# A token mixer and a mixture of experts on one core: the mixer cut into rounds of four tiles, with the first part of the shared expert inside it

## The chip, the cores and the metric

The kernel runs on one core of a Trainium2 chip. The metric is the device time of one launch in microseconds (us). Inputs and the output lie in DRAM, and all numbers are 32-bit floats. The engines are TensorE (PE, matmuls and transposes into the eight PSUM banks), VectorE (DVE), ScalarE (ACT), GpSimd (POOL) and SyncE (SP), which here only issues transfers. Each engine runs its own list of instructions in the order in which the program wrote them, and waits on semaphores.

## The reference, cut to what matters

Two sequences of 1024 tokens (16 tiles of 128 tokens) with 512 features pass through two layers.

```python
h = layernorm(x) * (1 + ca) + sa
x_shift = (roll(h, -T//2) @ Wts.T) * g + h * (1 - g)
xn = layernorm(x_shift) * ln_w + ln_b
k, v = xn @ Wk.T, xn @ Wv.T
wkv = exp(-exp(time_first) * sigmoid(k)) * v
states: s = s * exp(time_decay) + wkv          # a scan over the tokens
x = x + ga * (states @ Wo.T)
h = layernorm(x) * (1 + cb) + sb
shared = (silu(h @ Wsg) * (h @ Wsu)) @ Wsd * sigmoid(h @ Wse)
# router: softmax(h @ Wr), best 4 of 32 experts per token, at most 64 tokens
# per expert; each expert is silu(xe @ Wg) * (xe @ Wu) @ Wd
x = x + gb * (shared + weighted sum of the token's expert rows)
```

The hidden width of the shared expert is 1408, that of one routed expert 352.

## The kernel before, in words

The program has two blocks, and no engine begins the second before the first has ended on all.

**The mixer block** takes one sequence (8 tiles) at a time. First come eight `mixer` products (L884: 12 matmuls each, since a 32-bit product is made of three products of high and low parts in the fp32r type), and behind each `mix_front` on DVE (L723, then statistics L690 to L696), a power on POOL (L378), the normalization L713, a transpose on PE (L837), its copy on ACT (L467) and the low part on DVE (L594). Two `keys_values` products of 12 matmuls each (L899) and two scans (`kv_scan`, L732 and L734) follow. Then come eight `project` products (L923) with `residual` on DVE (L740, L690 to L696, L749), a scaling on ACT (L502), an addition on POOL (L404) and a transpose. `router` (L915) makes the logits of four tiles at a time. The second sequence repeats this.

**The expert block** runs 16 `UNITS` (p, g) in order: part p of the shared expert's width (2, 3, 3 and 3 chunks of 128) for group g of four tiles. A unit is, for each chunk, `gate_up` (24 matmuls, L1557) with silu on ACT (L1241) and a product on DVE (L1432), then four `down` products (L1570: 9 matmuls for three chunks, 6 for two) with two DVE instructions each (L1453, L1456). In unit 0 DVE also picks the experts; PE then counts the places (`positions`, L1640 and L1641) and DVE makes the indices (`slots`, L1384 to L1409) and signals `route_ok`. POOL writes 64 columns of token numbers by indirect transfers (L1181), SP reads the table back (L1123), and POOL gathers the rows of the first pair of experts (L1188). The 16 pairs have three stages each on PE: `pair_rows` and `pair_gate_up` (L1589, L1601: 32 matmuls), `pair_turned` (L1607), `pair_down` (L1618: 12 matmuls). One stage stands behind each chunk and each down of units 5 to 11 (`stage_after`), 49 places for 49 stages. A pair's weights lie in one buffer each: SP loads `egu` (four transfers of 704 KB, L1108) when the pair before has done `pair_gate_up`, then `ed` (two of 512 and two of 192 KB, L1112 and L1113) when it has done `pair_down`, then stores the pair's output `ye` (256 KB, L1136) and waits for that store (L1138) before it looks at the next pair. The last four units run beside the gather and sum of the experts' rows, which POOL issues (L1206).

## Time and profile before

| | us |
|---|---|
| median of 3 runs (lowest, highest) | 864.04 (861.78, 864.19) |
| span of the profiled execution | 815.9 |
| PE busy in it | 705.4 |
| DVE busy in it | 433.8 |
| POOL busy in it | 287.8 |
| ACT busy in it | 219.7 |

No time of its own is recorded for the profiled execution beside its span; the median run is 48.1 us longer than the span, which is what lies ahead of the first instruction and behind the last. A busy PE is not PE at its peak: the records of matmuls overlap, and they are longer where the granted clock is lower.

### The profile page before, as it was taken

What the parts mean: (1) busy time and instruction counts of PE and PEld (TensorE: products, weight loads), DVE (VectorE), ACT (ScalarE), POOL (GpSimd) and SP (SyncE); (2) the same over time, 40 slices, a digit from 0 to 9 for tenths busy, and PEclk for the clock granted to TensorE, in tenths of its full rate; (3) what the DMA queues carried; (4) which work ended last, traced back from release to release, by engine and by line L of the source; (5) the groups of instructions that cost most, each with busy time, mean ns of one, the idle gap of its engine ahead of it and who ended that gap; (6) DMA issues with size and microseconds to landing.
All of it is one profiled execution on the core that took longest, in us unless ns stands there. A gap on an engine that the chain in (4) does not pass through costs nothing.

```text
span 815.9 us, 8820 instructions
## 1 busy us (share of the span) xinstructions
PE 705.4 (86%) x3153; PEld 478.0 (59%) x3153; DVE 433.8 (53%) x749; ACT 219.7 (27%) x402; POOL 287.8 (35%) x272
## 2 busy tenths in 40 slices
PE   5798687978874899937999999999999999896995
PEld 3666534852252676825666566657566666674773
DVE  2888587647378766620323234241413234677777
ACT  2423423123241223301213132222223241322420
POOL 0184636813322377760000000000000002888881
PEclk9799756978697999977999999999999999998998
DMA  8610011021130430003685858668876763521111
GB/s 283 252 56 1 0 40 64 1 77 39 64 117 0 140 75 1 0 14 135 233 319 181 308 163 297 252 225 312 314 271 224 268 224 108 151 70 40 39 41 64
DMA packets 50487, 111.49 MB, mean 137 GB/s; under 512 B 11392, under 2 KB 15508, under 8 KB 50444
## 3 DMA queue, kind: packets, MB, share of 16 engines
q1 hardware_dynamic: 41996, 102.48, 35.6%
q0 software_dynamic: 8448, 8.46, 3.9%
q8 instruction: 25, 0.41, 0.2%
q14 instruction: 18, 0.15, 0.1%
HBM read 110.84 MB, written 12.62 MB: 151 GB/s over the span
## 4 chain that ended last, share of the span: by engine, by line
PE 38%; POOL 11%; DVE 9%; issue 8%; DMA 4%; ACT 1%; SPq 1%; POOLq 0%; DVEq 0%; ACTq 0%
PE bank L1557 16%; PE bank L1601 9%; POOL slot_tokens L1181 7%; PE bank L1570 6%; PE bank L1618 5%; POOL egu L1206 2%; DMA egu<-in_L_ffn_Wu_dram 2%; DVE ytmp L1470 1%; PE bank L1589 1%; DMA expert_rows<-ye 1%; DMA xg<-h_rows,slot_tok 1%; DVE xsL L1425 1%; DVE egu L1366 1%; DVE prod L1432 1%; PE bank L1607 1%
## 5 line engine op out<-in xcount | busy, mean ns | idle before, releaser
L1557 PE MATMUL bank<-xsH,wguH 128*128 128x512 f32 x352 | 142.3, 404 | 9.1 <-DVE xsL L1425 6.7
L1557 PE MATMUL bank<-xsH,wguL 128*128 128x512 f32 x352 | 138.5, 393 | 0.0
L1557 PE MATMUL bank<-xsL,wguH 128*128 128x512 f32 x352 | 138.4, 393 | 0.0
L1188 POOL DMA_INDIRECT xg<-h_rows,slot_tok x16 | 16.0, 999 | 273.5 <-PE bank L1589 270.5
L1432 DVE TENSOR_TENSOR prod<-bank,silu 128x512 f32<-128x512 f32 x44 | 30.4, 690 | 154.0 <-PE bank L1557 142.0
L1570 PE MATMUL bank<-wdH,prodH 128*128 128x512 f32 x176 | 75.1, 427 | 28.7 <-DVE prodL L1434 14.5
L1557 PEld LDWEIGHTS bank<-xsH,wguH 128*128 128x128 f32 x352 | 67.1, 191 | 30.8 <-issue 7.8
L1181 POOL DMA_INDIRECT slot_tokens<-tok_id,t_idx x64 | 67.8, 1060 | 43.1 <-DVE slotw L1409 23.9
L1601 PE MATMUL bank<-egu,xeT 128*64 128x352 f32 x512 | 79.3, 462 | 1.8 <-DMA egu<-in_L_ffn_Wu_dram 1.7
L1557 PEld LDWEIGHTS bank<-xsL,wguH 128*128 128x128 f32 x352 | 66.8, 190 | 14.5
L1557 PEld LDWEIGHTS bank<-xsH,wguL 128*128 128x128 f32 x352 | 67.0, 190 | 13.7 <-issue 0.7
L1570 PE MATMUL bank<-wdL,prodH 128*128 128x512 f32 x176 | 70.7, 402 | 0.0
L1570 PE MATMUL bank<-wdH,prodL 128*128 128x512 f32 x176 | 70.7, 402 | 0.0
L1243 ACT ACTIVATE prodH<-prod 128x512 fp32r<-128x512 f32 x44 | 27.8, 631 | 134.0 <-DVE prod L1432 134.0
L1570 PEld LDWEIGHTS bank<-wdH,prodH 128*128 128x128 f32 x176 | 34.3, 195 | 47.1 <-DVE prodL L1434 17.4
L1601 PEld LDWEIGHTS bank<-egu,xeT 128*64 128x64 f32 x512 | 36.6, 137 | 40.7 <-issue 32.9
L1241 ACT ACTIVATE silu<-bank 128x512 f32<-128x512 f32 x44 | 26.3, 597 | 120.4 <-PE bank L1557 120.2
L1206 POOL DMA_INDIRECT egu<-expert_rows,y_idx x44 | 50.0, 1136 | 19.5 <-issue 12.1
L1453 DVE SCALAR_TENSOR_TENSOR ytmp<-bank,sigma,gate_b 128x512 f32<-128x512 f32 x48 | 35.9, 747 | 31.0 <-PE bank L1570 30.7
L884 PE MATMUL bank<-wtsH,hT 128*128 128x512 f32 x128 | 47.1, 430 | 0.0
L1434 DVE TENSOR_TENSOR prodL<-prod,prodH 128x512 fp32r<-128x512 f32 x44 | 30.5, 692 | 30.7 <-ACT prodH L1243 30.7
L378 POOL TENSOR_TENSOR rs<-ve,neg_half 128x1 f32<-128x1 f32 x32 | 20.8, 651 | 69.7 <-DVE ve L696 69.7
(217 smaller groups left out, 1121.2 us busy)
## 6 DMA issues: line engine op xcount, KB each, us to landing
egu<-in_L_ffn_Wg_dram SPq DMA_DIRECT2D x32, 704.0 KB, 6.6
egu<-in_L_ffn_Wu_dram SPq DMA_DIRECT2D x32, 704.0 KB, 7.9
ed<-in_L_ffn_Wd_dram SPq DMA_DIRECT2D x32, 512.0 KB, 5.4
h2T<-in_L_wmod_dram SPq DMA_DIRECT2D x6, 1024.0 KB, 8.5
ed<-in_L_ffn_Wd_dram SPq DMA_DIRECT2D x32, 192.0 KB, 6.3
xres<-in_L_attn_x_dram SPq DMA_DIRECT2D x4, 1024.0 KB, 13.4
h_rows<-h2r SPq DMA_DIRECT2D x16, 256.0 KB, 2.0
expert_rows<-ye SPq DMA_DIRECT2D x16, 256.0 KB, 7.0
```

What stands on the lines that cost most here:

```text
L884: ins = m.matmul(sbk[i % 2][:, :], l[:, c, s * P:(s + 1) * P], r[:, c, :], start=(k == 0), stop=(k == 3 * C - 1))
L1181: gp.indirect_dma_start(tok_dram[:, :], bass.IndirectOffsetOnAxis(t_idx[:, i, k:k + 1], axis=0), tok_id[:, i:i + 1], None, bounds_check=E ...
L1206: gp.indirect_dma_start(yg[i % NY][:, k, :], None, ye_dram[:, :], bass.IndirectOffsetOnAxis(y_idx[:, i, k:k + 1], axis=0), bounds_check=E ...
L1241: a.activation(silu[:, :], gB[:, :], ACT.Silu).then_inc(silu_ok, 1)
L1243: a.activation(prodH[:, f, :], prod[:, :], ACT.Copy).then_inc(phi_ok, 1)
L1432: v.tensor_tensor(prod[:, :], uB[:, :], silu[:, :], ALU.mult).then_inc(prod_ok, 1)
L1434: v.tensor_tensor(prodL[:, f, :], prod[:, :], prodH[:, f, :].bitcast(F32), ALU.subtract).then_inc(plo_ok, 1)
L1453: v.scalar_tensor_tensor(ytmp[:, m % 2, :], dB[m % 2][:, :], sigma[:, i:i + 1], gate_b[:, i // BT, :], ALU.mult, ALU.mult).then_inc(d_used ...
L1557: ins = mm.matmul(bk[:, :], l[:, w, c, at], r[:, c, :], start=(k == 0), stop=(k == 3 * C - 1))
L1570: ins = mm.matmul(dB[m % 2][:, :], l[:, f, m * P:(m + 1) * P], r[:, f, :], start=(f == 0 and k == 0), stop=(f == nf - 1 and k == 2))
L1601: ins = mm.matmul(bk[half, 0:F], xeT[:, c, half], egu[:, e, w, c, :], start=(c == 0), stop=(c == C - 1))
L1618: ins = mm.matmul(eyB[half, :], epT[0:n, c, half], ed[0:n, e, c, :], start=(c == 0), stop=(c == len(FC) - 1))
```

## The change

The two blocks become one. The mixer runs in five rounds g of four tiles: round g has the `mixer` products of group g (rounds 0 to 3) and, step by step between them, the `project` products of group g - 1 (rounds 1 to 4); a round ends with `keys_values(g)` and `router(g - 1)`. Units (0, 0) to (0, 2) of the shared expert stand in rounds 2, 3 and 4 (`early_piece`). All products of the mixer share two PSUM banks in turn, so a `mixer` product of rounds 1 to 3 waits until DVE has taken the one before it. `keys_values` is 4 plain fp32 matmuls on undivided operands, which drops the 16 low parts of `xnT` on DVE. The router's operands change sides (16 matmuls of 34 columns), so that the logits come with tokens on partitions. A chunk of a unit is cut into halves of 12 matmuls. The pairs' 49 stages are spread over 44 places from unit 7, place 6, to the end of unit 11. SP asks for the third part's weights ahead of the scatter and not behind it. Buffers of the mixer and of the experts lie over each other, with waits that keep them apart.

```text
unit:    0-2          3          4 5 6    7 ... 11            12-15
before:  after mixer  --------   5 to 11: 49 stages           sum of rows
after:   in rounds    routing    scatter  7 (place 6) to 11   sum of rows
```

```diff
-    PAIR_UNIT = NG + 1
+    EARLY = NG - 1
...
-                    def keys_values(b, n):
...
-                        for c in range(C):
-                            for l, r in ((kvH, xnTH), (kvH, xnTL), (kvL, xnTH)):
-                                ins = m.matmul(kvb[:, :], l[:, c, :], r[:, c, :], start=(k == 0), stop=(k == 3 * C - 1))
-                                k += 1
-                        ins.then_inc(kv_full, 1)
...
-                if u < PAIR_UNIT:
-                    return None
-                n = sum(steps(UNITS[w][0]) for w in range(PAIR_UNIT, u)) + k - 1
-                j, stage = n // 3, n % 3
...
-                    load_part(1)
-                    sp.wait_ge(route_ok, 1)
-                    load_gate_up(0)
-                    load_down(0)
-                    sp.wait_ge(scat, 16 * NT * TOP_K)
...
-                        if j == 0:
-                            load_part(2)
-                        if j == NP // 2 + 1:
-                            load_part(3)
...
+        PAIRS_FROM = (7, 6)
+        PLACES = [(u, k) for u in range(PAIRS_FROM[0], MERGE) for k in range(2 * PARTS[UNITS[u][0]] + GT)
+                  if (u, k) >= PAIRS_FROM]
+        STAGES = 3 * NP + 1
+        stages_at = {}
+        for s in range(STAGES):
+            stages_at.setdefault(PLACES[s * len(PLACES) // STAGES], []).append(divmod(s - 1, 3))
...
+                sp.wait_ge(route_ok, 2)
+                load_gate_up(0)
+                load_down(0)
+                load_part(2)
+                sp.wait_ge(scat, 16 * NT * TOP_K)
+                sp.dma_start(slot_tok[:, :], tok_dram.rearrange("(p j) a -> p (j a)", p=P)).then_inc(tab_in, 16)
...
+                for g in range(NG + 1):
+                    for i in range(GT):
+                        t = g * GT + i
+                        if g < NG and 1 < t + 1 < NT:
+                            h_lo(t + 1)
+                        if g > 2 and i == 0:
+                            down(0, g - 3, 2)
+                            down(0, g - 3, 3)
+                        if g > 1 and i == 0:
+                            lo_group(0, g - 2)
+                            sigma_of(g - 2)
+                        if 2 <= g < NG and i in (1, 2):
+                            gate_up(0, g - 2, i - 1)
+                        if 2 <= g < NG and i == 3:
+                            down(0, g - 2, 0)
+                            down(0, g - 2, 1)
+                        if g == NG and i == 2:
+                            gate_up(0, g - 2, 0)
+                        if g < NG:
+                            mix_front(t)
+                        if g:
+                            residual(t - GT)
+                        if g < NG:
+                            mix_norm(t)
...
+                    for f in range(n):
+                        pair_stages(u, 2 * f)
+                        gate_up(p, g, f)
+                        if u == EARLY and f == 0:
+                            top_experts()
+                        if u == EARLY and f == 1:
+                            experts_mask()
+                        if f == 0 and g == 0 and p:
+                            for k in weights_ahead(u - 1)[2:]:
+                                lo_weights(p, k)
+                            lo_weights(p, n)
+                        if u == POOL_UNIT and f == 0:
+                            positions()
+                            slots()
+                        if u == POOL_UNIT and f == 1:
+                            slot_weights()
+                        pair_stages(u, 2 * f + 1)
...
+                def keys_values(g):
+                    k = product_bank(("kv", g))
+                    for i in range(GT):
+                        turn_taken(pe, ("xn", g * GT + i))
+                    if g == 0:
+                        pe.wait_ge(kvW_ok, C)
+                    for c in range(C):
+                        ins = mm.matmul(s_bank[k][:, :], kvW[:, c, :], xnT[:, c, :], start=(c == 0), stop=(c == C - 1))
+                    ins.then_inc(s_full[k], 1)
...
+                    for i in range(GT):
+                        turn_taken(pe, ("h2", g * GT + i))
+                        for c in range(C):
+                            ins = mm.matmul(s_bank[k][:, i * R:(i + 1) * R], h2T[:, g, c, i * P:(i + 1) * P], wrN[:, c, :],
+                                            start=(c == 0), stop=(c == C - 1))
...
+                    if k < 2 * NC0:
+                        half(0, g, k // 2, k % 2)
+                    else:
+                        down(0, g, k - 2 * NC0)
...
+                for g in range(NG + 1):
+                    for i in range(GT):
+                        t = g * GT + i
+                        for q in before_mixer(g, i):
+                            turn(q)
+                        if g < NG:
+                            mixer(t)
+                        if g:
+                            project(t - GT)
+                        if 2 <= g < NG:
+                            early_piece(g - 2, 2 * i)
...
+                            vector_product(i + 3)
+                        for q in amid(g, i):
+                            turn(q)
+                        if 2 <= g < NG:
+                            early_piece(g - 2, 2 * i + 1)
+                        for q in after_step(g, i):
+                            turn(q)
+                        if g == 0:
+                            vector_columns(i + 3)
+                    if g == NG:
+                        for k in range(GT, 2 * GT):
+                            early_piece(g - 2, k)
+                    for q in before_end(g):
+                        turn(q)
+                    if g < NG:
+                        keys_values(g)
+                    for q in at_end(g):
+                        turn(q)
+                    if g:
+                        router(g - 1)
...
+                    for f in range(n):
+                        half(p, g, f, 0)
+                        pair_stages(u, 2 * f)
+                        half(p, g, f, 1)
+                        pair_stages(u, 2 * f + 1)
+                    for m in range(GT):
+                        down(p, g, m)
+                        pair_stages(u, 2 * n + m)
```

Three places of the order in which the engines' instructions now stand. First DVE, one step of a mixer stage; before, a step of the second sequence (`mix_front`, the normalization of the tile before, a low part):

```order
L723 TENSOR_TENSOR xs<-bank,mix 128x512
L690 BN_STATS st<-xs 128x6
L695 BN_AGGR mv<-st 128x2
L696 TENSOR_SCALAR ve<-mv 128x1
L713 TENSOR_SCALAR xn<-xs,mv,rs 128x512
L594 TENSOR_TENSOR xnTL<-bank,xnTH 128x4x128
```

After, the second step of round 2 (`gate_up` of the shared expert, `mix_front`, `residual`, the normalization `mx`):

```order
L1100 TENSOR_TENSOR silu<-bank,silu 128x512
L1102 TENSOR_TENSOR prodL<-silu,prodH 128x512
L1022 TENSOR_TENSOR mx<-bank,mx 128x512
L1024 BN_STATS st<-mx 128x6
L1027 BN_AGGR mvx<-st 128x2
L1028 TENSOR_SCALAR vex<-mvx 128x1
L1039 TENSOR_TENSOR xres<-bank,xres 128x512
L1041 BN_STATS st<-xres 128x6
L1045 BN_AGGR mvh<-st 128x2
L1046 TENSOR_SCALAR veh<-mvh 128x1
L1056 SCALAR_TENSOR_TENSOR ho<-xres,mvh,bc 128x512
L1033 TENSOR_SCALAR mx<-mx,mvx,rsx 128x512
```

Each step now holds a tile of both stages and a piece of the shared expert, and the low part of `xnT` (L594 on `xnTL`) is gone.

Second DVE, where it makes the experts' places; before, behind the last downs of unit 0:

```order
L1453 SCALAR_TENSOR_TENSOR ytmp<-bank,sigma,gate_b 128x512
L1456 TENSOR_TENSOR xres<-xres,ytmp 128x512
L1384 TENSOR_TENSOR ed<-bank,egu 128x16x32 x4
L1387 TENSOR_REDUCE pos<-ed 128x64
L1389 TENSOR_SCALAR over<-pos 128x64
```

After, at the start of unit 4 (L1100 and L1102 are `gate_up` of its first chunk, L1082 and L1086 low parts of weights, L1173 the first of `positions`):

```order
L1121 SCALAR_TENSOR_TENSOR ytmp<-bank,sigma,gate_b 128x512
L1124 TENSOR_TENSOR xres<-xres,ytmp 128x512
L1082 TENSOR_TENSOR wguL<-wguN,wguH 128x1024
L1100 TENSOR_TENSOR prod<-bank,silu 128x512
L1102 TENSOR_TENSOR prodL<-prod,prodH 128x512
L1082 TENSOR_TENSOR wguL<-wguN,wguH 128x1024
L1086 TENSOR_TENSOR wdL<-wdN,wdH 128x512 x3
L1173 TENSOR_TENSOR ed<-bank,egu 128x16x32 x4
L1176 TENSOR_REDUCE egu<-ed 128x64
```

Compared with before, the places are now made behind the first chunk of the next unit and further low parts of weights.

Third ACT, around the decay factors of a group (L492 to L495 before); before:

```order
L467 ACTIVATE xnTH<-bank 128x4x128 x5
L492 ACTIVATE kE<-bank,kvbias 64x512
L493 ACTIVATE vV<-bank 64x512
L495 ACTIVATE kE<-kE,wcol 64x512
L467 ACTIVATE xnTH<-bank 128x4x128 x3
```

After, from the end of round 2 into round 3:

```order
L704 ACTIVATE kE<-bank,kvbias 64x512
L705 ACTIVATE vV<-bank 64x512
L707 ACT_TABLE_LOAD
L707 ACTIVATE kE<-kE,wcol 64x512
L684 ACTIVATE h2T<-bank 128x4x128
L667 ACTIVATE bc<-bank 128x512 x2
L717 ACTIVATE logits<-bank 128x136
L723 ACTIVATE sigma<-logits 128x4
L672 ACTIVATE hT<-bank 128x512
L754 ACTIVATE xsH<-h2T 128x512 x4
L762 ACT_TABLE_LOAD
L762 ACTIVATE silu<-bank 128x512
```

A table load now stands between `vV` and the exponential, and another ahead of each round's first silu.

## Rows read from the trace of the kernel before

**Rows 1.** Stretches: length, busy PE, PEld, DVE, ACT, POOL, clock, DMA share, GB/s.

```profile
0.00:31.00 31.00, 19.92 (x102) 14.47 (x102) 13.95 (x39) 10.39 (x19) 1.92 (x9) 0.86 0.91 317
31.00:85.00 54.00, 48.76 (x278) 36.88 (x276) 44.82 (x103) 17.22 (x33) 27.78 (x25) 0.95 0.13 41
85.00:133.00 48.00, 36.64 (x97) 20.74 (x98) 34.60 (x62) 17.43 (x30) 26.22 (x23) 0.56 0.08 28
133.00:177.00 44.00, 35.49 (x168) 28.58 (x169) 32.58 (x61) 10.25 (x17) 29.07 (x27) 0.89 0.16 54
177.00:224.30 47.30, 41.37 (x92) 15.57 (x92) 21.71 (x42) 13.99 (x23) 15.12 (x16) 0.72 0.12 45
224.30:275.60 51.30, 33.63 (x129) 24.44 (x130) 43.20 (x105) 12.51 (x20) 10.35 (x15) 0.87 0.14 47
275.60:372.60 97.00, 73.64 (x312) 57.23 (x311) 49.84 (x71) 23.76 (x39) 68.79 (x65) 0.92 0.25 70
372.60:687.20 314.60, 311.81 (x1549) 198.12 (x1550) 101.98 (x147) 80.85 (x171) 18.52 (x16) 0.99 0.68 240
687.20:815.90 128.70, 104.14 (x432) 81.95 (x432) 91.10 (x122) 33.30 (x54) 90.00 (x77) 0.94 0.23 68
```

**Rows 2.** POOL in time: first scatter, first gather.

```profile
275.57 1.25 POOL L1181 DMA_INDIRECT slot_tokens<-tok_id,t_idx  x1 [23.88 <-DVE slotw L1409]
...
365.54 1.00 POOL L1188 DMA_INDIRECT xg<-h_rows,slot_tok  x1 [2.96 <-DMA slot_tok<-slot_tokens]
```

**Rows 3.** PE in time: start us, length us, what; in brackets idle before.

```profile
372.66 1.13 PE L1589 MATMUL bank<-ident,xg 128*128 128x128 f32 x4 [19.47 <-DMA xg<-h_rows,slot_tok]
```

**Rows 4.** The chain that ended last: start us, length us, what.

```profile
262.19 1.71 PE bank L1640 x2
...
265.65 2.49 DVE ed L1384 x4
...
365.54 7.07 DMA xg<-h_rows,slot_tok
...
380.97 4.88 PE bank L1601 x32
...
406.98 2.07 PE bank L1570 x9
409.05 2.73 PE bank L1618 x12
412.46 5.49 PE bank L1557 x24
```

**Rows 5.** DVE groups by form: busy us, mean ns, then idle before.

```profile
L1453 DVE SCALAR_TENSOR_TENSOR ytmp<-bank,sigma,gate_b 128x512 f32<-128x512 f32 x48 | 35.9, 747 | 31.0 <-PE bank L1570 30.7
...
L723 DVE TENSOR_TENSOR xs<-bank,mix 128x512 f32<-128x512 f32 x16 | 11.0, 689 | 13.0 <-PE bank L884 12.6 <-POOL mix L391 0.3
...
L740 DVE TENSOR_TENSOR xres<-bank,xres 128x512 f32<-128x512 f32 x16 | 11.0, 686 | 10.0 <-PE bank L923 9.9
```

**Rows 6.** PE in time, a router product of four fp32 matmuls.

```profile
188.01 3.62 PE L915 MATMUL bank<-h2T,wrN 128*34 128x512 f32 x8
```

**Rows 7.** ACT groups: the table load ahead of the silu.

```profile
L1241 ACT ACT_TABLE_LOAD x1 | 1.3, 1283 | 0.0
```

**Rows 8.** SP's issues in time, one cycle of pair weights.

```profile
446.08 0.34 SPq L1108 DMA_DIRECT2D egu<-in_L_ffn_Wg_dram  x1
...
454.72 0.65 SPq L1136 DMA_DIRECT2D expert_rows<-ye  x1
462.81 0.34 SPq L1108 DMA_DIRECT2D egu<-in_L_ffn_Wg_dram  x1
```

**Rows 9.** PE in time, the pair that waits for its weights.

```profile
456.80 3.47 PE L1601 MATMUL bank<-egu,xeT 128*64 128x352 f32 x22 [1.51 <-DMA egu<-in_L_ffn_Wu_dram]
```

**Rows 10.** The page's 40 slices (20.4 us each): granted clock, GB/s.

```profile
PEclk9799756978697999977999999999999999998998
...
GB/s 283 252 56 1 0 40 64 1 77 39 64 117 0 140 75 1 0 14 135 233 319 181 308 163 297 252 225 312 314 271 224 268 224 108 151 70 40 39 41 64
```

2457 lines of the change are left out of this document (1205 added, 1252 removed).

## The prediction

> **What bounds the kernel now.** I read the stretches first, since four parts of the program have different limits. The mixer block takes 224.3 us, and no engine is full in it: DVE is busy 44.82 of 54 us while the first sequence is mixed, but only 34.60 of 48 and 21.71 of 47.3 in the two `project` stretches, and the granted clock falls to 0.56 there [rows 1]. PE and DVE wait for each other along one chain. Next comes routing, 51.3 us, which is DVE's. Then POOL scatters: from 275.57, when it has waited for DVE's last index, to the first gather at 365.54 [rows 2]. PE has finished units 1 to 4 by then and sits idle 19.47 us until the gathered rows land at 372.66 [rows 3]. The pairs take 314.6 us, 311.81 of them with PE busy and a full clock [rows 1]. The last 128.7 us are POOL's gathers (90.00 us busy) with PE at 104.14.
>
> Check of the PE-bound part by counting: 24 matmuls of a chunk take 5.49, nine of a down 2.07, 32 of `pair_gate_up` 4.88, 12 of `pair_down` 2.73 [rows 4]. A three-chunk unit is 3 x 5.49 + 4 x 2.07 = 24.8; a pair with its transposes (about 1.2) is 8.8. From 372.66 before had two chunks, four downs, six units and 16 pairs: 19.3 + 148.8 + 141 = 309, against 314.6 measured. So the counting holds to 2%.
>
> **The change, part by part.** I follow four points of time: M, the end of the last router product (224.3 before, taken as the end of the mixer stretch [rows 1]); the first gathered rows on PE; the last `pair_down`; the end.
>
> *M.* Work that moves in: three units of part 0 (72 matmuls, 16.4 us of PE each, 49 in all), and on DVE 12 low parts at about 0.7, 12 products and low parts of `gate_up`, 12 downs of two instructions and the weights' low parts, 38 us at about 0.7 each [rows 5]; 16 low parts of `xnT` at about 0.7 go, so +27. DVE was busy 147.7 us up to 224.3 (sum of the first five lines of [rows 1]); it would be 175. At the old density (0.66) M would be 265, at the 0.83 of the best stretch 211. By steps: round 0 is half of the old 54 us, from 31 to 58. Its end then lies open: `keys_values` in fp32 (four matmuls as in [rows 6], 3.6 instead of 2.7), the decay factors, the scan, the gate columns: 12, so 70. Round 1: a step has about 17 DVE instructions, at the 0.435 mean and 0.83 density of the 54 us stretch 8.9 each, so 105. Rounds 2 and 3: PE's step is a mixer product (2.74), a projection (0.9, one fp32 matmul as in [rows 6]), two halves (5.5) and transposes (1), 10.2; the two steps with downs are DVE's, 9 each. Between rounds PE goes through `keys_values`, transposes and the router product (3.6 each, [rows 6]) and DVE through scan, downs and low parts before the next `mix_front`; I count 12 to 15 us per round end, so 50 and 53 per round: 155, 208. Round 4 has no mixer, eight pieces of 16.4 us behind four projections, and two products at its ends: 46. M = 254, bounds 240 (PE's work alone at full clock, with no wait at the ends) and 272.
>
> *Table loads.* The order shows eight instead of two. One takes 1.28 us [rows 7]. Those ahead of the silu fall into ACT's wait for a gate product; two stand between `vV` and the exponential, on the chain of the scan: 2.6, inside the 53s. The Trainium skill (ScalarE: Activation LUTs, "What ACT_TABLE_LOAD costs") gives about 2.66 us per switch, drain included. The trace shows only the 1.28; by the page six further switches, all exposed, would cost 16.
>
> *M to the first gathered rows.* Before, 372.66 - 224.3 = 148.4. Up to `positions` the chain keeps its length (the block's start and the logits' copies go, a low part comes). Before, DVE began the places at 265.65 [rows 4] and POOL scattered at 275.57 [rows 2]. After, DVE first needs both halves of unit 4's first chunk (5.5), their product, high and low part (2.2), and four low parts (3.4): about 11, less 1.2 for `slotw`, which now comes later. So +10. Against it, part 2's weights no longer stand in front of the first gather, whose landing took 7.07 [rows 4]; I take 2.5 for it, -4.6. So +5.6, bounds 0 and +10. PE has units 4 to 6 and most of 7 to do meanwhile, 74 + 18.5 from M + 41, and the rows come at M + 154: it idles about 17, much as before. Moving the pairs to unit 7 therefore costs nothing here.
>
> *The pairs.* What is left for PE from there: three downs of unit 7 (6.2), units 8 to 11 (99), 16 pairs (141): 246. But `pair_gate_up` must start every 15.6 us on average (14.2 to 16.9 by the places), where before it was 19.7. SP's cycle of one pair, where it was packed, ran from 446.08 to 462.81 [rows 8]: the load of `egu`, 10.7 us until PE could start at 456.80 after a wait of 1.51 [rows 9], 4.95 of matmuls, and the wait for the store of `ye`, issued at 454.72 behind `ed`. So 16.7 is the period that the single buffers and SP's order allow. A pair moves 4736 KB (4.85 MB); at the best slice, 319 GB/s [rows 10], that is 15.2. I take 16.3 where PE would be faster: +13 over 15 periods, and +2 for part 3's weights. Pairs 261, bounds 246 (PE) and 272 (16.7 throughout, and 7 for part 3). Gain 314.6 - 261 = 53.6.
>
> The Trainium skill (DMA: Bandwidth & Descriptors, "Bandwidth") puts the ceiling of the SBUF side at 435 GB/s, by which the bytes of a pair need 11.1 us and PE stays the bound, 246 and not 261. No slice here shows more than 319, over 20 us; whether the ceiling is reached inside one is not in these rows.
>
> *The tail.* POOL's gathers follow the last store of `ye` and are not touched: 128.7.
>
> *Sum*, against the span of 815.9: M +29.7, routing +5.6, pairs -53.6, tail 0: -18.3. The span becomes 797.6. The median of the runs is 48.1 above the span, which nothing here changes: 864.0 - 18.3 = 846.
>
> **The rivals.**
>
> *A, faster still.* Pairs at PE's pace (-15) or M at its lower bound of 240 (-14), each alone 831, both 817. For it: DMA share is only 0.68 in the pairs [rows 1], and PE's pieces fill the mixer's waits, so the clock may stay high. Against it: a wait of PE for `egu` is already there at a period of 15.7 [rows 9]. The ceiling rule above would give 831. Chance 0.20.
>
> *B, slower.* The mixer's rounds lock step: each `mixer` product waits for DVE to empty its bank, DVE waits for a projection behind it, and PE's in-order pieces stand in front of the transposes that POOL and DVE wait for. If each of the 12 steps and four round ends of rounds 1 to 4 takes 2.2 us more than I count, M is 289 and the time 881; slower begins at M = 275, 1.3 us each. For it: DVE's density of 0.66 in the old mixer gives 265 with a simpler order. Against it: in the 54 us stretch DVE and PE ran at 0.83 and 0.90 together with such a chain. Chance 0.20.
>
> *C, table loads.* If every one of the six lies on a chain, 6 x 1.28 = 7.7, of which 2.6 are counted: 851; by the skill's 2.66 it would be 859. Chance 0.05.
>
> *D, it comes out even.* The pairs' periods reach only 17.5 (SP late at each store), +18 over 15 periods, with the rest as forecast: 864. Chance 0.07.
>
> **How the numbers follow.** The forecast has 0.48, with its own range of 836 to 857. The range of 8 in 10 reaches to 826 (half of A lies below 831) and to 870 (about half of B beyond). A measurement tells 0.3%, 2.6 us, from no change: faster takes the forecast, A, C and a third of D, 0.75; same 0.05; slower 0.20.
>
> **What would show it.** Right: the last router product at 240 to 272 in the new profile, with DVE at about 0.7 of that stretch; first scatter 60 us or so behind it; PE's wait for `xg` of 10 to 25; `pair_gate_up` starting every 16 to 17 us, with several waits for `egu`; tail 127 to 131. Wrong: M above 275 (B); no wait for `egu` and pairs of 246 (A); ACT's table loads in the chain more than twice (C); SP's waits for the store longer than 8 (D). A tail of another length would break the sum where I put nothing.

## The result, and the profile after

The changed kernel takes 888.61 us (median of four runs, 886.71 to 901.44), the kernel before 863.33: 1.0291 times as long, 95% interval 1.0272 to 1.0309. The longest of the four, a disturbed run, is left out of the ratio. The change makes the kernel slower by 25 us, where 18 less was forecast.

The stretches of the changed kernel's profiled execution (888.17 us, span 886.3), cut at the last router product (M), the first scatter, the first gather, the first gathered rows on PE and the last `pair_down`. They answer to [rows 1]:

```profile
core 0: us, PE busy (x) PEld busy (x) DVE busy (x) ACT busy (x) POOL busy (x), PEclk, DMA share, GB/s
0.00:279.30 279.30, 223.03 (x1029) 159.70 (x1029) 172.82 (x347) 91.08 (x155) 96.01 (x92) 0.88 0.21 73
279.30:341.10 61.80, 40.25 (x137) 29.80 (x138) 44.59 (x104) 16.66 (x27) 7.79 (x13) 0.79 0.00 1
341.10:427.60 86.50, 35.77 (x138) 27.78 (x138) 16.51 (x28) 9.36 (x17) 64.20 (x64) 0.70 0.34 78
427.60:484.60 57.00, 50.67 (x214) 41.45 (x215) 25.44 (x37) 12.25 (x21) 1.00 (x1) 0.91 0.02 5
484.60:758.90 274.30, 251.99 (x1271) 145.79 (x1269) 72.34 (x107) 63.90 (x144) 17.71 (x16) 0.97 0.77 275
758.90:886.30 127.40, 103.98 (x432) 81.97 (x432) 92.60 (x124) 33.21 (x56) 88.70 (x77) 0.94 0.23 69
```

Two things stand out. M is 279.3, not 254. And in the 86.5 us of the scatter PE gets 138 matmuls done, where in the profile before it got 312 done; then it has 50 us of the shared expert left when the gathered rows are there.

The timeline of the scatter (POOL, ACT and DVE rows in order of time; in brackets the engine's idle time before, and its releaser, "remote" where none in the program is found):

```profile
341.12 1.24 POOL L606 DMA_INDIRECT slot_tokens<-tok_id,t_idx  x1 [34.47 <-DVE t_idx L1191]
...
381.80 0.60 ACT L762 ACTIVATE silu<-bank 128x512 f32<-128x512 f32 x1 [11.92 <-remote]
...
412.66 0.69 DVE L1100 TENSOR_TENSOR prod<-bank,silu 128x512 f32<-128x512 f32 x1 [42.03 <-remote]
...
423.55 0.97 POOL L606 DMA_INDIRECT slot_tokens<-tok_id,t_idx  x1 [0.30 <-issue]
427.61 1.00 POOL L613 DMA_INDIRECT xg<-h_rows,slot_tok  x1 [3.09 <-DMA slot_tok<-slot_tokens]
...
432.96 0.75 DVE L1121 SCALAR_TENSOR_TENSOR ytmp<-bank,sigma,gate_b 128x512 f32<-128x512 f32 x1 [17.02 <-remote]
```

ACT takes the gate product of a chunk at 381.80; DVE can take its `up` product, 12 matmuls later in PE's order, only at 412.66: 30.9 / 12 = 2.6 us per matmul of 512 columns, where [rows 4] have 5.49 / 24 = 0.23. The first down ends 15 matmuls further on, at 432.96, 9 us behind the issue of the last scatter. The granted clock can't be the cause: 2.6 is eleven times 0.23, and at the lower of its two levels (0.50 from 341.5 to 345.3 us) these matmuls follow each other by 0.43. I call this the slow stretch. It is the subject of half the experiments, since it hides what the change does.

### The profile page after: what moved, and what is told of

Read it like the earlier page. It is cut to its first block, busy times and chain, and to the rows that moved or that the text cites. A ratio compares the mean times of both kernels' runs of the same rounds, so it can differ in the third digit from the quotient of the medians.

```text
span 886.3 us, 8906 instructions
## 1 busy us (share of the span) xinstructions
PE 705.7 (80%) x3217; PEld 486.5 (55%) x3217; DVE 424.3 (48%) x745; ACT 226.5 (26%) x418; POOL 275.4 (31%) x263
## 4 chain that ended last, share of the span: by engine, by line
PE 40%; DVE 15%; DMA 14%; issue 10%; another core or an unknown queue 7%; POOL 6%; ACT 4%; SPq 3%; POOLq 0%; DVEq 0%; ACTq 0%
PE bank L1478 16%; DMA egu<-in_L_ffn_Wu_dram 7%; PE bank L1533 6%; DMA expert_rows<-ye 6%; PE bank L1490 6%; PE bank L1428 3%; PE bank L1550 3%; PE bank L1439 2%; POOL egu L631 2%; DMA xres<-in_L_attn_x_dram 1%; DVE ytmp L1212 1%; PE bank L1459 1%; DVE prod L1100 1%; SPq L458 1%
## 5 line engine op out<-in xcount | busy, mean ns | idle before, releaser
L1478 PE MATMUL bank<-xsH,wguH 128*128 128x512 f32 x352 | 144.9, 412 | 16.3 <-DVE xsL L1092 9.4
L1490 PE MATMUL bank<-wdH,prodH 128*128 128x512 f32 x176 | 77.0, 438 | 81.3 <-issue 39.9
L613 POOL DMA_INDIRECT xg<-h_rows,slot_tok x16 | 15.2, 949 | 289.0 <-PE bank L1521 285.9
L1100 DVE TENSOR_TENSOR prod<-bank,silu 128x512 f32<-128x512 f32 x38 | 26.2, 691 | 160.1 <-PE bank L1478 95.7
L1533 PE MATMUL bank<-egu,xeT 128*64 128x352 f32 x512 | 84.6, 486 | 19.8 <-DMA egu<-in_L_ffn_Wu_dram 17.5
L1478 PEld LDWEIGHTS bank<-xsH,wguH 128*128 128x128 f32 x352 | 67.8, 193 | 44.2 <-issue 20.2
L606 POOL DMA_INDIRECT slot_tokens<-tok_id,t_idx x64 | 64.2, 1003 | 53.7 <-DVE t_idx L1191 34.5
L1490 PE MATMUL bank<-wdH,prodL 128*128 128x512 f32 x176 | 72.8, 413 | 0.0
L1533 PEld LDWEIGHTS bank<-egu,xeT 128*64 128x64 f32 x512 | 38.0, 144 | 62.4 <-issue 37.1
L768 ACT ACTIVATE prodH<-prod 128x512 fp32r<-128x512 f32 x38 | 24.0, 631 | 156.7 <-DVE prod L1100 146.5
L1205 DVE TENSOR_TENSOR eprod<-bank,esilu 128x352 f32<-128x352 f32 x16 | 8.4, 525 | 105.1 <-ACT esilu L778 105.1
L1428 PE MATMUL bank<-wtsH,hT 128*128 128x512 f32 x128 | 49.9, 454 | 2.5 <-DVE wtsL L939 1.7
L1550 PE MATMUL bank<-ed,epT 128*64 128x512 f32 (+1 forms) x192 | 44.8, 600 | 0.9 <-issue 0.9
```

Source lines behind the costliest of these rows:

```text
L606: gp.indirect_dma_start(tok_dram[:, :], bass.IndirectOffsetOnAxis(t_idx[:, i, k:k + 1], axis=0), tok_id[:, i:i + 1], None, bounds_check=E ...
L768: a.activation(prodH[f][:, :], src[:, :], ACT.Copy).then_inc(phi_ok, 1)
L1100: v.tensor_tensor(to[:, :], uB[:, :], silu[:, :], ALU.mult).then_inc(prod_ok, 1)
L1428: ins = mm.matmul(s_bank[k][:, :], l[:, c, :], r[:, c, :], start=(n == 0), stop=(n == 3 * C - 1))
L1478: ins = mm.matmul(bk[:, :], l[f][:, w, c, :], r[:, c, :], start=(k == 0), stop=(k == 3 * C - 1))
L1490: ins = mm.matmul(dB[m % 2][:, :], l[f][:, m * P:(m + 1) * P], r[f][:, :], start=(f == 0 and k == 0), stop=(f == nf - 1 and k == 2))
```

## The experiments

Ratios are to the kernel before, run beside it on the same chip, with 95% intervals. The experiments ran on four chips, so two of them from different chips are compared by these ratios and not by their times. Where a stretch is given, it is from the run's own profile, one execution. How far that can be trusted, M shows: in the seven profiles of the changed kernel in which nothing ahead of M is altered it lies between 277.3 and 282.8.

### Where the 48 us outside the span were

**before_again**: the kernel before, unchanged.

> The kernel before, unchanged, to see in one execution both its span and its own time. The changed kernel's execution lay 1.9 us outside its span (888.17 against 886.3), while for the kernel before 48 us were left over between a span of 815.9 and runs of 864. Theory 1 (the profile shown of before was an execution in which TensorE was not held up while the scatter ran, and the timed runs have such a stretch): a span of about 861 us here, 1.9 us below its own time, with a hold-up of TensorE of some 45 us between the first scatter and the first gathered rows. Theory 2 (the 48 us really lie outside the span of this kernel): a span of about 816 us beside a time of about 864.

862.43 us, ratio 0.9986 [0.9957, 1.0014]; its profiled execution took 864.01 with a span of 862.2. Theory 1. Its stretches from M on (columns as above):

```profile
223.10:275.20 52.10, 33.62 (x129) 24.46 (x130) 43.21 (x105) 13.12 (x21) 10.37 (x15) 0.87 0.14 46
275.20:360.20 85.00, 24.02 (x90) 17.81 (x89) 11.28 (x17) 5.36 (x10) 62.86 (x64) 0.68 0.20 52
360.20:421.30 61.10, 54.25 (x222) 42.85 (x223) 37.34 (x52) 17.76 (x28) 1.00 (x1) 0.92 0.13 44
421.30:733.90 312.60, 309.49 (x1550) 196.33 (x1548) 103.31 (x149) 81.41 (x171) 18.53 (x16) 1.00 0.68 241
```

Only 90 matmuls run in the scatter, and the pairs begin at 421.3, where [rows 3] have 372.66. The profile shown of before was of an execution without the slow stretch; the timed runs, by their times, have it. So my 48.1 us "outside the span" were 1.8 us outside it and 46 of slow stretch. Against this execution the change reads: M +56.2, routing to the first scatter +9.7, scatter and the work behind it -2.6, pairs -38.3, tail -0.9: +24.1.

### What the slow stretch is

**part2_late**: the third weight group is loaded behind the slot table's read.

```
-                load_part(2)
                 sp.wait_ge(scat, 16 * NT * TOP_K)
                 sp.dma_start(slot_tok[:, :], ...)
+                load_part(2)
```

> The changed kernel with the load of the shared expert's third group of weight columns moved on SyncE from ahead of the read of the slot table to behind it, so that its 2.3 MB are not under way while the scatter runs. In the changed kernel three products of TensorE in the scatter ended 10, 31 and 15 us late, from the moment that these transfers ended. Theory 1 (the hold-up comes with these transfers): it is gone, first gathered rows are used at about 434 instead of 484, time about 840 us. Theory 2 (it has to do with the scatter itself or with TensorE's own activity): the hold-up of 50 to 60 us stays, time 885 to 892.

889.98, 1.0303 [1.0253, 1.0352]: nothing changes (138 matmuls in the scatter again), theory 2.

**half_scatter**: `for i in range(NT // 2)` around the scatters, so the second sequence's tokens get no slot.

> The changed kernel that leaves out the last 32 of the 64 scatters, so the second sequence's tokens are in no slot (their experts' part is not computed; the gathers read other rows in their place, with the same number of transfers). The scatter ends 41 us earlier. Theory 1 (TensorE is held up until the scatter is over): the slow stretch, which begins 30 us behind the first scatter, lasts to about 392 instead of 433, TensorE reaches the pairs at about 444 instead of 484, and the time is 843 to 850. Theory 2 (the slow stretch has a length of its own and only falls into the scatter): no change of it, time 884 to 890.

847.32, 0.9808 [0.9740, 0.9876]. The last scatter is issued at 381.5 instead of 423.6, and PE is at the pairs at 436.0 instead of 484.6, with the same 138 matmuls done between the first scatter and the first gather. Theory 1: the slow stretch ends with the scatters.

**scatter_paced**: four semaphores in turn, and a wait on the one four places back.

```
+                        q = i * TOP_K + k
+                        if q >= 4:
+                            pool.wait_ge(scats[q % 4], 16 * (q // 4))
                         gp.indirect_dma_start(tok_dram[:, :], ...).then_inc(scats[q % 4], 16)
```

> The changed kernel with the 64 scatters of the slot table paced: each waits on GpSimd until the one four places ahead of it has landed, so at most four are under way. All five executions looked at except the one shown of the kernel before have a stretch behind the first 20 to 30 us of the scatter in which TensorE gets one product of 512 columns done in about 2.5 us, two scatters' time, where it takes 0.23. Theory 1 (what holds TensorE up are scatters that pile up unfinished): the products run at 0.23 throughout, TensorE reaches the pairs when the rows land, at about 435, and the time is 838 to 845. Theory 2 (the issuing of a scatter itself, or something else of that time, holds it up): unchanged, 885 to 892, or a little longer if the scatters take longer.

Three runs at 878 to 881 and one at 863. PE gets 203 matmuls done in the scatter and then has the slow stretch: neither theory as it stood, but the pacing moves it.

**scatter_by_two** and **before_by_two**: the same with two in place of four, on either kernel.

> The changed kernel with at most two of the 64 scatters under way (with four, TensorE's slow stretch began 44 us behind the first scatter instead of 30, and one run of four came out at 863). Theory 1 (unfinished scatters are what holds TensorE up): no slow stretch, some 290 products in the scatter instead of 137, pairs begin when the rows land, and the time is 838 to 850, by how much longer the 64 scatters take. Theory 2 (pacing does not matter, and where the stretch begins is chance): 875 to 895, with the slow stretch.

> The kernel before with the same pacing, at most two scatters under way. Theory 1 (the hold-up is the same thing in both kernels, and the execution shown of before was one without it): 815 to 830, that is 15 to 24 us faster than the changed kernel paced alike, so the change's own effect is there without the hold-up too. Theory 2 (the hold-up stays): 855 to 870.

863.65, 0.9957 [0.9922, 0.9991], and 835.47, 0.9650 [0.9587, 0.9713]. The slow stretch is gone in both. The stretch of the scatter in scatter_by_two, columns as above:

```profile
344.70:458.50 113.80, 82.83 (x351) 66.99 (x351) 43.46 (x67) 23.85 (x40) 64.91 (x64) 0.86 0.21 60
```

PE does 351 matmuls, runs out of work and waits 34 us, as the 64 scatters now take 110 us instead of 82. Both times lie above the ranges I gave (838 to 850 and 815 to 830), and I had expected 15 to 24 us between the two, where there are 28. But theory 1 holds, and without the slow stretch the change costs as much as with it. One thing these runs leave open: with two under way the scatters are also issued more slowly, one per 1.74 us instead of 1.31 in the mean, and no run separates the number under way from the rate.

### The pairs

**pairs_early**: `PAIRS_FROM = (6, 6)` instead of `(7, 6)`.

> The changed kernel with the pairs' first stage 10 places earlier in the list of turns, (6, 6) instead of (7, 6), so 54 places for 49 stages. In the changed kernel TensorE comes to the first pair at 484.6, 57 us after the gather was issued at 427.6, with 50 us of the shared expert still ahead of the pairs. Theory 1 (the order keeps the pairs back after a hold-up): the first rows are used some 20 us earlier, at about 462, and of TensorE's 22 us of idle time in the pairs some 5 to 10 go, time 878 to 884. Theory 2 (pairs are bound by their transfers and the tail takes what is saved): no change, 886 to 890. If the hold-up is absent in this execution TensorE waits for the gather instead, and the time is about 840.

870.05 (ten runs, 863 to 885), 1.0036 [0.9999, 1.0072]. The first rows are used at 463.5 (21 earlier), the pairs take 278.1. Theory 1, and more than the 5 to 11 us that its range allowed: with the slow stretch the late start of the pairs leaves PE idle in the pairs (251.99 busy of 274.30 above), with the earlier one it is 271.12 of 278.10.

**sp_order**: SyncE waits for a pair's store behind the next `load_gate_up`.

```
                         load_gate_up(j + 1)
+                    if j:
+                        sp.wait_ge(ye_sent, 16 * j)
+                        sp.sem_inc(ye_free, 1)
...
-                    sp.wait_ge(ye_sent, 16 * (j + 1))
-                    sp.sem_inc(ye_free, 1)
```

> The changed kernel with SyncE waiting for the store of an expert pair's rows one place later, behind the issue of the next pair's gate and up weights instead of ahead of it. In the changed kernel SyncE waits 116 us in all for these stores and TensorE 17.5 us in all for the weights. Theory 1 (the weights come late since SyncE stands at the store): TensorE's wait for them falls below 6 us, and the pairs take 8 to 12 us less, 876 to 880. Theory 2 (the weights are late because TensorE asks for them in bursts and the transfers are at what the memory gives): no change, 885 to 890.

889.32, 1.0293 [1.0236, 1.0350]. The pairs take 262.1 instead of 274.3, as theory 1 says (PE's wait for `egu` falls to 8.0, not below 6); the total does not move, since PE came to the pairs at 494.8. Nothing ahead of that differs in the order of any engine's work, and yet the slow stretch began earlier: 95 matmuls in the scatter instead of 138.

**combo**: (6, 6), this order of SyncE, and two edits of the mixer told below.

> The changed kernel with four edits together: pairs from (6, 6), SyncE's later wait for the store, the order of round 1, and the rows ahead in round 2. The stretches that these moved when made alone: M -5.8 (round 1's order), 0 to -6 (rows ahead), pairs 274.3 to 262.1 (SyncE's wait), and 17 us by the earlier pairs. Theory 1 (they add up as far as TensorE has idle time left; it has 7 us in the pairs with the earlier start): M at 268 to 273, the pairs 272 to 276, time 855 to 862, even with the kernel before or a little faster. Theory 2 (the slow stretch in the scatter gives it back, as it did in the two runs with one edit): 868 or more.

869.34, 1.0017 [0.9988, 1.0047]; theory 2. 107 matmuls in the scatter. From here on I paced by two.

**combo_by_two**: this order of SyncE and round1_order below, `PAIRS_FROM` unchanged.

> The changed kernel with at most two scatters under way, the order of round 1 and SyncE's later wait for the store. Made alone these took 5.8 us from M and 12.2 from the pairs, and neither run was faster, since the slow stretch in the scatter began 10 us earlier in both. Theory 1 (that was chance): without the slow stretch both come through, 863.65 - 18 = 846, range 843 to 849. Theory 2 (something downstream takes back what they give, such as the last transfers or the tail): 855 or more.

843.25, 0.9757 [0.9712, 0.9802], against 0.9957 for scatter_by_two: theory 1, both gains come through (M 272.9, pairs 260.7). PE's waits in its pairs (total, times, longest):

```profile
PE bank L1531 <- DMA xg<-h_rows,slot_tok: 35.2, 1, 35.2
PE bank L1543 <- DMA egu<-in_L_ffn_Wu_dram: 5.7, 4, 4.2
```

The waits of PE and of SyncE's queue in the changed kernel's pairs, where PE's wait for `egu` was 17.5:

```profile
PE bank L1533 <- DMA egu<-in_L_ffn_Wu_dram: 17.5, 9, 9.2
...
SPq L491 <- DMA expert_rows<-ye: 114.1, 15, 12.6
```

### The mixer

**no_pieces**: none of the shared expert in the rounds, its first three units behind the mixer. One unit's low part is made of another group's rows here, so its part of the output is not the reference's; the operations are the same in kind and number.

> The changed kernel with none of the shared expert's first part inside the mixer's rounds: its first three units are computed behind the mixer, with the fourth, and the routing's vector work stands beside units 0 and 1; the load of the third group of columns stands behind the read of the slot table. The three units take 72 products each, 3 x 72 x 0.227 = 49 us of TensorE. Theory 1 (the rounds are bound by TensorE's order of work, and the pieces cost there what they cost alone): the last router product ends at 279 - 49 = 230. Theory 2 (the rounds are bound by the chain through VectorE, ScalarE and GpSimd from step to step, and the pieces lie in its gaps): it ends at 260 or later. In between, each us of pieces cost (279 - M)/49. As the same work stands behind the mixer, the whole is 886 to 895 with the hold-up of TensorE in the scatter, and about 840 to 850 without it.

932.53, 1.0796 [1.0746, 1.0845]. M is 259.2: taking 49 us of PE's work out gives back 20, so about 30 of the 49 lay in gaps; between the theories. The total is beyond both, as the slow stretch took the time in which PE would have done this work.

**no_pieces_by_two**: the same, with each group's own rows, paced.

> The changed kernel with at most two scatters under way and with the shared expert's first three units behind the mixer instead of in its rounds. Beside scatter_by_two (863.65; M at 282.8, first scatter at 344.7, TensorE idle for 34 us before the gathered rows, pairs at 462). Theory 1 (the pieces cost nearly half their own 49 us in the rounds, and TensorE could do them in its idle time under the scatter): M at 259, first scatter at about 315, rows at about 435, TensorE busy until about 445, pairs from there: 845 to 850, faster than with the pieces. Theory 2 (the pieces in the rounds pay): TensorE comes to the pairs later than 462, and the time is 865 or more.

859.50, 0.9950 [0.9921, 0.9980], beside 0.9957 for scatter_by_two. M 262.2, first scatter 318.2, PE at the pairs at 458.1 against 462.0. Neither theory: the time is the same, since PE had 27 us left behind the gather, where I had reckoned 10. With the scatters paced, running the pieces beside the mixer is worth nothing: what PE saves there it idles away under the scatter. Unpaced it was worth 44 us (932.5 against 888.6).

**round1_order**: on DVE the statistics ahead of the weights' low parts, on POOL `first_rstd` behind `mix_rows`.

```
-                            if i < NC0 + 1:
-                                first_lo(i)
                             for q in FIRST[2 * i:2 * i + 2]:
                                 first_stats(1, q)
...
+                            if i < NC0 + 1:
+                                first_lo(i)
```

> The changed kernel with two places of round 1 in another order: on VectorE a step's statistics of the second sequence come ahead of the low parts of the shared expert's first weights, so that ScalarE's copy of those weights (1.8 to 1.9 us of VectorE's waiting, three times) lies beside them; on GpSimd the power of the second sequence's variances comes behind mix_rows and h2_rows instead of ahead of mix_rows (VectorE waited 3.2 us for mix_rows there). Theory 1 (round 1 is bound by one chain through VectorE and GpSimd, and such waits stand on it): 5 to 8 us shorter up to the last router product, 271 to 274 instead of 279, time 880 to 884. Theory 2 (the chain only waits elsewhere): no change, 886 to 890.

Round 1, from its first sum to its last norm, takes 37.9 us instead of 46.9, and the end of the round behind it is no longer than before. M is 273.5 (5.8 less, and below all seven profiles with the old order), theory 1; the total, 892.84, 1.0273 [1.0202, 1.0345], is lost to a longer slow stretch (83 matmuls in the scatter).

**rows_ahead**: `first_rows` ahead of `mix_front` in round 2.

> The changed kernel with VectorE writing the second sequence's normalised rows ahead of mix_front in the steps of round 2, instead of behind mix_norm. In round 2 TensorE's turn ('h', t + 1) waits for these rows, which wait for mix_norm(t), which waits for TensorE's mixer product of t, so the two engines take turns. Theory 1 (this turn-taking sets the step of round 2): round 2, from the keys and values of group 1 to those of group 2, takes 50 to 54 us instead of 57.4, and the last router product ends at 273 to 276. Theory 2 (TensorE's pieces set it): 57 us and 279. The whole moves by as much, if the slow stretch in the scatter begins where it did.

901.27, 1.0408 [1.0344, 1.0472]; round 2 takes 57.2 us (57.4 without the edit), M is 283.5. Theory 2. So the turn-taking of DVE and PE within a step does not set the pace of round 2.

**router_late**: the router's products of groups 0 and 1 behind the next round's first mixer product (paced).

> The changed kernel with at most two scatters under way and the router's products of groups 0 and 1 one place later in TensorE's order, behind the first mixer product of the next round instead of ahead of it. Theory 1 (VectorE's first sum of rounds 2 and 3 is late since the mixer product stands behind 32 products of the router, 6.7 us, of TensorE): the gaps from the last norm of a round to the first sum of the next shrink from 20.2 and 27.9 by 3 to 6 us each, M by 5 to 10, time 854 to 859 beside 863.65. Theory 2 (TensorE is full there, and what is moved comes back in the step behind): the gaps shrink but M moves by less than 3.

870.01, 1.0076 [1.0046, 1.0106], 1.2% above scatter_by_two's 0.9957. The gap from round 2's norm to round 3's sum falls from 27.9 to 20.5, and the step behind it grows from 9.0 to 17.4; M is 289.0, where 282.8 was without the edit. Theory 2, and worse.

**front_first**: DVE's `mix_front` ahead of the low parts and the downs at the rounds' starts (paced).

> The changed kernel with at most two scatters under way and VectorE's first step of rounds 2 and 3 in another order: mix_front first, then the low parts of the piece's group and sigma, then the two downs that were left, then residual and mix_norm (before: downs, low parts, sigma, mix_front, residual, mix_norm). Theory 1 (the next round's first sum waits for what stands ahead of it on VectorE): the gap from round 2's last norm to round 3's first sum falls from 27.9 to about 24.5, M from 282.8 to 277 to 280, time 858 to 861 beside 863.65. Theory 2 (TensorE's order sets the pace there, and the pieces' first half now starts later): the gap falls, the step behind grows by as much, M and time move by less than 2.

870.05, 1.0051 [1.0014, 1.0088], 0.9% above scatter_by_two. The gap falls to 24.8, the step grows to 14.8; M is 285.1. Theory 2 again, and slower.

### A version that beats both

**before_late_pairs**: before_by_two with the pairs' 49 stages from unit 6 on, and the SyncE order above.

> The kernel before with at most two scatters under way, the pairs' 49 stages spread from the third place of unit 6 (two units and two places of work of TensorE are then ahead of the first pair instead of one unit) as the changed kernel spreads them, and SyncE's later wait for the store. Beside before_by_two (835.5, TensorE idle for 39 us before the gathered rows). Theory 1 (TensorE has the work for its idle time, and the pairs then run at the transfers' pace of 16.4 us each): pairs start at about 390 and take 270 to 280 instead of 314, time 795 to 805. Theory 2 (the denser pairs wait for transfers): pairs take 290 or more, 812 to 825.

829.65, 0.9585 [0.9508, 0.9661]. Theory 2: the pairs take 308.8, and the time lies above even that theory's 812 to 825. PE is idle for 26.5 us of them, 17.8 for `egu` (not the 40 that the next expectation names).

**before_fine_pairs**: with the changed kernel's places, one behind each half of a chunk.

```
+            PLACES = [(u, k) for u in range(6, NG * (len(PARTS) - 1))
+                      for k in range(2 * PARTS[UNITS[u][0]] + GT) if (u, k) >= (6, 4)]
...
-                            pair_stage(u, f)
+                            pair_stage(u, 2 * f + 1)
```

> before_late_pairs (829.65; pairs 308.8 us, of which TensorE waited some 40) with the places of the pairs' stages as the changed kernel has them: one behind each half of a chunk and one behind each down, ten in a unit, from the fifth of unit 6. Theory 1 (with one place behind a whole chunk, 5.5 us of products, several stages of a pair fall together, so that TensorE asks for weights in bursts): the pairs take 262 to 276, time 790 to 800. Theory 2 (the transfers' pace beside the mixer of before is what it is): the pairs stay above 300, time 825 to 832.

804.47, 0.9268 [0.9219, 0.9316]. Its stretches from the first scatter on, cut as before:

```profile
274.60:387.40 112.80, 106.59 (x456) 84.23 (x455) 63.45 (x91) 31.41 (x52) 68.81 (x64) 1.00 0.14 40
387.40:394.50 7.10, 0.00 (x0) 0.00 (x0) 0.00 (x0) 0.00 (x0) 1.00 (x1) 0.55 0.98 338
...
394.50:679.10 284.60, 278.57 (x1396) 168.05 (x1396) 85.67 (x124) 73.05 (x157) 18.52 (x16) 0.99 0.74 265
679.10:808.00 128.90, 108.33 (x442) 85.60 (x441) 93.54 (x124) 33.30 (x54) 89.86 (x77) 0.93 0.22 68
```

PE is busy 106.59 of the 112.80 us of the scatter and 278.57 of the 284.60 of the pairs, so they are PE's again, not the transfers'. Theory 1, somewhat short of it (262 to 276 for the pairs and 790 to 800 in all were expected). The old mixer, paced scatters, SyncE's later wait and the changed kernel's way of spreading the pairs are together 7.3% faster than before.

## Why the prediction was wrong

**The sum.** 846 was forecast, 888.6 measured: 42.6 too low. M +25.3 (279.3 for 254); M to the first gathered rows +51.3 (205.3 for 154); pairs +13.3 (274.3 for 261); tail -1.3 (127.4 for 128.7); outside the span -46.2 (1.9 for 48.1). The second and the last are the same thing, the slow stretch, counted in the profile on one side and outside the span on the other: they nearly cancel, +5.1. That is luck: I took 46 us of slow stretch for a constant, and the changed kernel happens to have one of its own. What turned the sign is M, and the pairs with it.

**M = 254, the step that failed.** The steps can be set beside the profile with DVE's first sum (L1022) of a round and the last norm (L1033):

```profile
56.46 1.48 DVE L1033 TENSOR_SCALAR mx<-mx,mvx,rsx 128x512 f32<-128x512 f32 x1 [0.66 <-POOL rsx L529]
...
71.76 0.69 DVE L1022 TENSOR_TENSOR mx<-bank,mx 128x512 f32<-128x512 f32 x1 [1.36 <-PE bank L1428]
...
118.08 0.54 DVE L1033 TENSOR_SCALAR mx<-mx,mvx,rsx 128x512 f32<-128x512 f32 x1
...
138.84 0.69 DVE L1022 TENSOR_TENSOR mx<-bank,mx 128x512 f32<-128x512 f32 x1 [0.51 <-PE bank L1428]
...
175.42 0.54 DVE L1033 TENSOR_SCALAR mx<-mx,mvx,rsx 128x512 f32<-128x512 f32 x1
...
203.90 0.69 DVE L1022 TENSOR_TENSOR mx<-bank,mx 128x512 f32<-128x512 f32 x1
...
234.43 0.54 DVE L1033 TENSOR_SCALAR mx<-mx,mvx,rsx 128x512 f32<-128x512 f32 x1
```

| | predicted | measured |
|---|---|---|
| end of round 0 | 58 | 57.9 |
| its end, to the first sum | 12 | 13.8 |
| round 1, four steps | 35 | 46.9 |
| round 1's end and round 2 | 50 | 20.2 + 37.1 |
| round 2's end and round 3 | 53 | 27.9 + 31.1 |
| round 4 | 46 | 44.3 |

The 25.3 us too few are round 1's steps (+11.9) and the three ends between rounds (+1.8, +8.2, +12.9), less 9.5 elsewhere: the steps of rounds 2 and 3 were forecast well or too long (38 each), and so was round 4. For round 1, "about 17 DVE instructions, at the 0.435 mean and 0.83 density" left out that DVE waits there for ACT's copies of the weights and POOL's powers; with these in another order its first steps came at 8.8 and 8.9 us instead of 10.7 and 13.4, its third at 15.5 instead of 18.0, and 9.0 of the 11.9 were gone (round1_order). And "12 to 15 us per round end" was 20 and 28. What fills the third, on DVE and then on PE (timeline of the changed kernel):

```profile
187.07 0.74 DVE L1062 SCALAR_TENSOR_TENSOR kE<-vV,kvbias,kE 64x512 f32<-64x512 f32 x1 [11.11 <-ACT kE L707]
187.85 1.22 DVE L1065 TENSOR_TENSOR_SCAN states<-wcol,kE 64x512 f32<-64x512 f32 x1
197.16 0.69 DVE L933 TENSOR_TENSOR hT<-bank,hT 128x512 fp32r<-128x512 f32 x1 [8.10 <-ACT hT L672]
...
201.09 2.49 DVE L1092 TENSOR_TENSOR xsL<-h2T,xsH 128x512 fp32r<-128x512 f32 x4
...
188.71 6.89 PE L1459 MATMUL bank<-wrN,h2T 128*128 128x34 f32 x32
195.40 1.09 PE L1379 MATMUL bank<-ident,xhat 128*128 128x128 f32 x4
```

DVE waits 11.11 for the decay factors and 8.10 for the next tile, whose transposes stand on PE behind 6.89 us of router product. I had counted 3.6 for it and 3.6 for `keys_values` [rows 6], and both take that at full clock (3.66 from 275.61 on, 3.67 from 236.94 on). But at the ends PE had just idled and the granted clock was at its lower level: 0.50 from 188.7 to 195.5, and 0.50 for the first 3 us of a `keys_values` of 5.60; at the other two ends it took 5.06 and 5.28. The ends between rounds, 13.8, 20.2 and 27.9, are where a mixer in rounds pays: without any pieces M is still 259 to 262, 36 to 39 above before. The pieces add 20. How much of the ends is clock and how much is order was not separated. Both attempts to shorten an end on one engine (router_late, front_first) came back in the step behind; both engines' orders would have to change, which I did not try.

**Rival B** put its limit at "slower begins at M = 275", with a chance of 0.20, and M came at 279. Its price for that M would be 871; the rest is the pairs and the slow stretch. Its mechanism came true in part: it spread the loss over all steps and ends alike, but the steps of rounds 2 and 3 lost nothing, and the ends and round 1 lost all of it. What spoke for it, DVE's density of 0.66 in the old mixer and M = 265 from it, was the better guide than my count by steps; it was 0.62 in the end (172.82 of 279.30). Rivals A and D did not come: A needed a shorter M or pairs at PE's pace, and had neither. D had the pairs nearly right (17.5 a pair), but with M as forecast.

**M to the first gathered rows.** First scatter +9.7 over before_again, +10 forecast. The first gather's landing, with part 2's weights no longer in front of it, was put at 2.5 instead of 7.1; in scatter_by_two it is 3.4 (458.53 to 461.96). PE's wait for `xg` of 17 (by the terms given there, 154 less 133.5, it should have read 20) never came; with pacing it is 34.

**The pairs.** 16.3 us per pair was forecast, 17.3 measured ((746.48 - 487.37) / 15). The step is "16.7 is the period that the single buffers and SP's order allow": the order was the limit, but SyncE's waits for the stores are 114.1 us in all, 7.6 each and up to 12.6, where before they were 100.1 and up to 8.1. It is not the slow stretch: without it the pairs take 274.4 (scatter_by_two). With the wait moved the period is 16.4 and the pairs take 261 to 262, which is what I had forecast with the wait in its old place. PE's own work in them, 246 by my count, is 248.6 to 252.0. The page rule I weighed, the Trainium skill's 435 GB/s ceiling (DMA: Bandwidth & Descriptors, "Bandwidth"), is not contradicted: cut into 6.9 us slices, the pairs show far more than the 319 of [rows 10], 401 at most. That bandwidth did not set the pace is shown by sp_order: the same bytes went in 262.1 us, at 287 GB/s instead of 275, by SyncE's order alone. The slices of the changed kernel's pairs:

```profile
GB/s 41 233 330 214 384 253 261 349 226 296 262 243 375 178 353 286 292 317 224 367 216 308 355 200 401 378 114 329 264 201 397 224 350 298 215 379 185 395 262 4
```

**Table loads.** Eight, as counted, two of them on the chain of the scan; ACT's timeline at the second:

```profile
241.35 0.59 ACT L705 ACTIVATE vV<-bank 64x512 f32<-64x512 f32 x1
241.96 1.28 ACT L707 ACT_TABLE_LOAD   x1
243.26 0.81 ACT L707 ACTIVATE kE<-kE,wcol 64x512 f32<-64x512 f32 x1
```

From the end of `vV` to the exponential pass 1.3 us, the load and nothing beside it. The Trainium skill (ScalarE: Activation LUTs, "What ACT_TABLE_LOAD costs") has 2.66 per switch; the trace shows half. In the chain that ended last only this one of the eight stands whole, so rival C, which wanted more than two, falls.

**The tail** was untouched, as said (127.4).

## What to carry to other kernels

Compare the profiled execution's span with the timed runs first. 46 us that lie between them are not "outside the span"; they may be a slow stretch that the profiled execution happened to lack, and every number of the stretch concerned is then of the wrong execution.

A pipeline in rounds is paid at the rounds' ends, where recurrence, in-order products and low parts meet. Count the ends one by one with every instruction that both engines have there, and at the lower clock if the engine idles there, before counting the steps. Overlapped work is worth only what no later idle time would have hidden.

Pace indirect transfers: a wait two places back made the scatter 25 to 27 us longer and both kernels 3.2 to 3.5% faster, as TensorE kept its pace. Give the time that TensorE then idles work by starting the later, transfer-bound stage later and spreading it finely.

## What the runs showed of the hardware

While up to 64 scatters of 128 four-byte rows were issued back to back, one per 1.28 us, TensorE's 512-column products slowed from 0.23 to 2.6 us from some point on, until about the end of the scatters. By the matmuls that TensorE got done while the scatters were issued, that point came early without pacing (78 to 138 matmuls), later with four under way (203) and never with two (351, all that it had). It differed between programs whose engines do the same up to there (138 and 95). Between the executions of one program the times often agree (885 to 887 in three spans of the changed kernel, 900 in a fourth), but not always: with four under way one of four runs took 863 and three 878 to 881, and pairs_early's ten lie between 863 and 885; whether the point of onset is what differs there is not shown. One execution of the kernel before, the first profile, did without it. The 2.3 MB of the third weight group are not the cause (part2_late), and with two scatters under way all weights are loaded where they were (scatter_by_two).

Why scatters that follow each other so fast hold TensorE up is not settled, nor whether their number under way or their rate does it. The Trainium skill (DMA: Bandwidth & Descriptors, "SWDGE vs HWDGE vs iDMA") places the rings of descriptors that GpSimd writes in SBUF, in two groups of 16 partitions. TensorE's operands here lie in 128 partitions; that the two accesses meet is not shown by any run here.
